# Six key-value iterations instead of seven, and the padding groups of edges at the end of a graph-transformer layer

## The chip, the cores and the metric

One core of a Trainium2 chip runs the whole layer as one program. Five engines work side by side: TensorE (PE, matmuls), VectorE (DVE), ScalarE (ACT), GpSimd (POOL, which here issues the gathers and scatters) and SyncE (SP, which issues plain transfers). The metric is the device time of one execution in microseconds, as the median of several runs.

## The reference

```
xn  = layernorm(x)                                   # 6250 nodes x 256
gnn = relu((relu(mean(xn[src] by dst) @ Wl.T + bl + xn @ Wr.T) @ Wln.T) + xn)   # 200000 edges
q, k, v = heads(xn @ w_qkv + b); k, v = layernorm(k), layernorm(v)     # 8 heads of 32
mix = gelu(((q @ (k.T @ v / 6250)) + xn) @ w1 + b1) @ w2 + b2 + xn
x   = x + gnn + mix
x   = x + shared_ffn(xn2) + top2_of_8_experts(xn2),  xn2 = layernorm(x)
```

The edges come sorted by destination, and low node numbers have more of them: in the inputs that `setup_inputs` draws, 40,621 of the 200,000 edges end in nodes 0 to 255, and 28,674 in nodes 0 to 127.

## The kernel before

**Tiles and groups.** The nodes are 49 tiles of 128 rows. The edges are cut into groups of 768 (6 columns of 128 edges); four groups, one for each buffer of `ring`, make an iteration, and 66 iterations cover 264 groups. The last edges, which belong to the highest nodes, are processed first. 261 groups hold real edges; three (`PADG`) hold only padding and are processed first, in iteration 0, from buffers set to zero.

**What a group costs.** POOL issues six indirect DMAs that gather 128 rows each of the normalised nodes `xn_d` into a ring buffer (`gather_edges`, L709). PE sums the rows by destination inside a window of 32 nodes (`window_sums`, L1734), DVE copies the sums (`keep_part`, L1223), PE places them in their tile (`place`, L1771), DVE adds them to the tile's sum (`finish`, L1158). When DVE has copied a group's sums it also copies the row numbers for a later gather (`next_rows`, L1231). A gather waits for that and, by the same register `group`, for `pass_`: the gather of group g may start when the sums of group g-3 are made.

**Stages.** First the node rows are normalised and stored to `xn_d`. In the *key-value stage* (`kv_iteration`, unrolled, iterations 0 to 6) each iteration handles four groups and seven node tiles, two tiles beside each of the first three groups and one beside the fourth (`SLOT`). A tile goes round ACT and DVE: ACT squares the projections (L843), DVE sums the squares (L1277), ACT takes the root, DVE the reciprocal and the product (L1283, L1286), ACT adds one (L831), PE multiplies keys by values (L1798). After tile 48 a short serial part makes the attention matrix (to L1433), and then the *node stage* starts, loops over iterations 7 to 65 on every engine.

**Node steps.** One iteration of the node stage does four groups and at most one *step* of the node work, which is a pipeline of steps 0 to 59: steps 0 to 51 finish one node tile after the other (SAGE, mixing, shared expert, from step 10 also pairs of row blocks of the routed experts), 52 is left out, step 53 opens the tables of the rest, and steps 54 to 59 do four single units of the routed experts each. A step may run only when no edge from this iteration on touches its tile: DVE makes a word for each iteration with the number of steps that are free, and `plan.look` sets `now` to the next step if its number is below that, and otherwise to `BLANK` (L93 to L96), which does nothing. With tile t the highest still touched, 48-t steps are free, three more when t is 1 or 0 and nine more when t is 0 (L1092 to L1095). After step 59 PE handles the last tile and its nine experts by itself.

**POOL's order.** In the node stage POOL's `step` issues, for each of the four buffers, the six gathers, and between them the step's two scatters of routed rows (L728) and two adds of expert results to the output (L737); for the single units one add for each buffer (L746). It is one queue in program order.

Of the kernel before, what the change touches and what calls it, by code (L numbers as in the profile page):

```python
# [8 lines left out]
ALU = mybir.AluOpType  # L9
# [4 lines left out]
ds = bass.ds  # L14

P = 128
NODES, D = 6250, 256
# [4 lines left out]
U = 6  # L22
RING = 4
KT = 7
KI = -(-NT // KT)
NKV = NT
SLOT = ((0, 1), (2, 3), (4, 5), (6,))
assert KI * KT == NT
NI = -(-EDGES // (P * U * RING))
# [3 lines left out]
SHELF = 8  # L33
# [168 lines left out]
def gps_layer(nc, x, idx, dst, wl, bl, wr, wln, wkv, bkv, wq, bq, kvg, kvb, w1, b1, w2, b2, wrt,  # L202
# [3 lines left out]
    with ctx:  # L206
# [216 lines left out]
        def rounds(it, b):  # L423

            return it if b < PADG else it + 1

# [30 lines left out]
        def _(sp):  # L457
# [8 lines left out]
            def first_lists():  # L466

                for b in range(RING):
                    sp.dma_start(idx_s[:, b, :], idx[RING * NI - 1 - b:RING * NI - b, :, :].squeeze(0)
                                 ).then_inc(S["idxin"], 16)  # L470

# [209 lines left out]
        def _(pool):  # L681
            nc.gpsimd.memset(ones_s[:, :], 1.0).then_inc(S["const"], 1)
            nc.gpsimd.memset(eps_s[:, :], EPS)
            nc.gpsimd.memset(zero_s[:, :], 0.0).then_inc(S["const"], 1)
            for b in range(PADG):
                nc.gpsimd.memset(ring[b][:, :, 0:D], 0.0)
            for b in range(RING):
# [11 lines left out]
            group = pool.alloc_register("group")  # L699
            pool.reg_mov(group, 2 + PADG)  # L700
            pool.sem_inc(S["idx"], RING + 1)
            pool.wait_ge(S["idxin"], 16 * RING)

            def gather_edges(b):
                pool.wait_ge(S["const"], 3)
                pool.wait_ge(S["idx"], group)
                pool.wait_ge(S["pass_"], group)
                for u in range(U):
                    pool.indirect_dma_start(  # L709
                        out=ring[b][:, u, 0:D], out_offset=None, in_=xn_d,  # L710
                        in_offset=IND(ap=idx_s[:, b, u:u + 1], axis=0)).then_inc(s_row[b], 16)
                pool.reg_add(group, group, 1)

            for b in range(PADG, RING):
                gather_edges(b)
            with pool.Fori(1, KI) as it:
# [32 lines left out]

            def step(gather):  # L750
                for b in range(RING):
                    if gather:
                        gather_edges(b)
                    if b == 1:
# [12 lines left out]
                with pool.If_lt(plan.single, plan.now):  # L767
                    pool.reg_add(units, units, 1)
# [11 lines left out]
            plan = Plan(pool, first=FIRSTS, second=SECONDS, add=ADDING, spread=SPREADING)  # L780
            with pool.Fori(KI, NI) as it:
                plan.look(word.now() >> RING)
                word.look_up(it + 1)
                step(True)
                plan.after()
            with plan.rest():
                with plan.left():
                    step(False)
                    plan.advance()
# [222 lines left out]
        def _(dve):  # L1012
# [27 lines left out]
            def extents():  # L1040

                dve.wait_ge(S["dstin"], 16)
                def pads_first(to):
                    V.tensor_copy(to[:, 0:2 * U], dst32_s[:, NG * U:])
                    return V.tensor_copy(to[:, 2 * U:], dst32_s[:, 0:NG * U])
# [21 lines left out]
            own.step(V.tensor_reduce(wide_s, span4_s, AX, ALU.max))  # L1067
            V.tensor_scalar(span_s[0:1, :], tile_i[0:1, :], 7, None, ALU.arith_shift_right).then_inc(S["span"], 1)
            dve.sem_inc(S["added"], 1)
# [29 lines left out]
            def pack(row, total, spare, terms):  # L1099
# [3 lines left out]
                for i, (part, factor) in enumerate(terms):  # L1103
# [104 lines left out]
            def enter_edges(edges):  # L1208

                finish(edges, -1)  # L1210
                state(edges, 1)
                narrow(edges, 1)
                with dve.If_eq(wide0, 1):
                    extra(at_group(edges[0], 0), edges[4][0])
                keep_part(edges, 0)
                dve.wait_ge(S["lists"], edges[0] * 16 + 16 * (len(SPANS) + 2 - SHELF))
                next_rows(edges[0] + 1, 0)
# [7 lines left out]
            def next_rows(it, b):  # L1225

                if isinstance(it, int):
                    at = shelf_of(it) * RING
                else:
                    at = dve.snap(shelf_of(it) * RING).with_bounds(min_val=0, max_val=(SHELF - 1) * RING)  # L1230
                V.tensor_copy(idx_s[:, b, :], lists_s[:, ds(at + (RING - 1 - b), 1), :].squeeze(1)).then_inc(S["idx"], 1)  # L1231

# [65 lines left out]
            def kv_iteration(it):  # L1298
                edges = begin(it)
                state(edges, 1)  # L1300
                for b in range(RING):
                    keep_part(edges, b)
                    next_rows(it + 1, b)
                    for j in SLOT[b]:
                        m = KT * it + j
                        if m:
                            scale(m - 1)
                        squares(m)
                        if j == SLOT[b][0] and (it, b) != (KI - 1, RING - 1):
                            finish(edges, b)  # L1310
# [404 lines left out]
        def _(pe):  # L1715
# [92 lines left out]
            def kv_iteration(it):  # L1808
                edges = begin(it)
                for b in range(RING):  # L1810
                    aggregate(edges, b)
                    for j in SLOT[b]:
                        m = KT * it + j
                        if m + 1 < NT:
# [4 lines left out]
                        if m >= 2:  # L1819
                            k_v(m - 2)  # L1820
                        if j == SLOT[b][0] and (it, b) != (KI - 1, RING - 1):
                            place(edges, b)
# [411 lines left out]
```

## Time and profile before

| | |
|---|---|
| median of 3 runs | 2538.97 us (2537.24 to 2541.27) |
| the profiled execution | 2541.11 us, of which 2539.1 us are its span |
| busy in the span | PE 2140.6 us (84%), POOL 1774.2 us (70%), DVE 1105.4 us (44%), ACT 769.8 us (30%) |
| gathers (L709) | 1566 DMAs, mean 956 ns |
| pieces of the gathers in the chain that ended last | POOL's issue 10%, the DMA itself 6% |

Busy time leaves out what an engine's sequencer does between instructions. A POOL that shows 70% can therefore still have a queue that never empties; the rows below show the idle time in front of each instruction, and what ended it.

### The profile page before, as it was taken

The numbers are of one execution on the slowest core, as the hardware profiler recorded it, in microseconds if no ns is written. First come the engines' busy times: TensorE is split into PE (matmuls) and PEld (weight loads), VectorE is DVE, ScalarE is ACT, GpSimd is POOL, SyncE is SP. The second block draws the span as 40 slices with busy tenths as digits, with TensorE's granted clock in tenths as the row PEclk, the third lists the DMA queues.
The fourth block names the chain that finished last, engine by engine and source line by source line (L and its number), as shares of the span: only waits on it lengthen the run. The fifth ranks groups of instructions, "written<-read, shape, count | busy, mean of one in ns | idle before, by whom it ended". The sixth has DMA issues, their size and how long they took to land.

```text
span 2539.1 us, 61133 instructions
## 1 busy us (share of the span) xinstructions
PE 2140.6 (84%) x13164; PEld 1655.5 (65%) x13165; DVE 1105.4 (44%) x4278; ACT 769.8 (30%) x1954; POOL 1774.2 (70%) x1786
## 2 busy tenths in 40 slices
PE   0888666777999999999999999999999866488979
PEld 0444445555777777777777777787777643377768
DVE  8555434444454445444444444444444322222321
ACT  4344222222233323323332333233333201022323
POOL 1477577777777777777777777777777777757720
PEclk9899778888999999999999999999999976599989
DMA  8333344445656665666566566656665654878834
GB/s 266 96 105 106 101 116 118 118 118 151 189 166 174 185 183 162 181 183 184 153 189 183 165 176 182 188 158 182 185 185 152 180 145 107 263 239 263 262 104 135
DMA packets 273733, 424.97 MB, mean 167 GB/s; under 512 B 76425, under 2 KB 202185, under 8 KB 272938
## 3 DMA queue, kind: packets, MB, share of 16 engines
q0 software_dynamic: 94880, 231.75, 33.6%
q1 hardware_dynamic: 172058, 183.19, 22.2%
q10 hardware_dynamic: 6384, 6.42, 0.7%
q14 instruction: 382, 3.13, 0.4%
q8 instruction: 29, 0.48, 0.1%
HBM read 380.74 MB, written 40.48 MB: 166 GB/s over the span
## 4 chain that ended last, share of the span: by engine, by line
PE 45%; issue 18%; POOL 13%; DVE 8%; DMA 7%; DVEq 4%; ACT 2%; SPq 1%; POOLq 1%; ACTq 0%
POOL region L709 10%; PE p_agg L1734 7%; PE p_y L1971 6%; DMA region<-xn_d,idx_s 6%; PE p_h L1960 4%; PE p_h L1927 4%; PE p_y L1933 4%; PE p_agg L1771 3%; PE p_h L2058 3%; PE p_a L2089 2%; PE p_t L1774 2%; PE p_a L1917 2%; POOL out_rows L737 2%; PE p_h L2123 1%; DVEq L171 1%
## 5 line engine op out<-in xcount | busy, mean ns | idle before, releaser
L709 POOL DMA_INDIRECT region<-xn_d,idx_s x1566 | 1497.3, 956 | 582.0 <-issue 447.6
L1734 PE MATMUL p_agg<-region,winhot 128*32 128x258 f32 x3168 | 318.0, 424 | 113.1 <-DMA region<-xn_d,idx_s 86.0
L1158 DVE TENSOR_TENSOR late<-late,p_agg 128x258 f32 x218 | 92.1, 423 | 514.9 <-issue 299.0
L1971 PE MATMUL p_y<-region 128*128 128x256 f32 x1280 | 293.5, 382 | 0.0
L1734 PEld LDWEIGHTS p_agg<-region,winhot 128*32 128x32 f32 x3168 | 120.3, 116 | 264.2 <-issue 197.9
L1771 PE MATMUL p_agg<-part_s,placehot 96*128 96x258 f32 x528 | 183.5, 431 | 119.7 <-DVE part_s L1223 95.7
L1971 PEld LDWEIGHTS p_y<-region 128*128 128x128 f32 x1280 | 240.1, 190 | 47.4 <-issue 16.6
L888 ACT ACTIVATE work<-p_h,b1s_s 128x128 f32<-128x128 f32 x384 | 109.7, 368 | 494.8 <-PE p_h L1927 494.8
L1960 PE MATMUL p_h<-wkv_s,region 128*128 128x256 f32 x960 | 229.2, 389 | 2.3 <-issue 2.2
L1960 PEld LDWEIGHTS p_h<-wkv_s,region 128*128 128x128 f32 x960 | 177.5, 191 | 40.8 <-issue 19.7
L1933 PE MATMUL p_y<-w2s_s,work 128*128 128x256 f32 x768 | 203.9, 390 | 0.0
L1927 PEld LDWEIGHTS p_h<-xft_s,w1s_s 128*128 128x128 f32 x1536 | 191.3, 200 | 11.0 <-issue 9.0
L1927 PE MATMUL p_h<-xft_s,w1s_s 128*128 128x128 f32 x1536 | 197.8, 284 | 0.0
L1771 PEld LDWEIGHTS p_agg<-part_s,placehot 96*128 96x128 f32 x528 | 91.1, 202 | 152.6 <-DVE part_s L1223 117.1
L1151 DVE TENSOR_TENSOR winhot<-row_s,iota_s 128x192 f32<-128x192 f32 (+1 forms) x265 | 95.1, 359 | 139.5 <-issue 131.6
L1933 PEld LDWEIGHTS p_y<-w2s_s,work 128*128 128x128 f32 x768 | 143.4, 197 | 18.3 <-issue 1.4
L737 POOL DMA_INDIRECT out_rows<-wkv_s,stok_s x80 | 130.0, 1625 | 24.4 <-issue 21.6
L870 ACT ACTIVATE region<-p_h,b_h 128x256 f32<-128x256 f32 x240 | 99.7, 471 | 151.0 <-PE p_h L1960 144.1
L1223 DVE COPY part_s<-p_agg 96x258 f32<-96x258 f32 x264 | 111.4, 422 | 62.2 <-PE p_agg L1734 47.8
L876 ACT ACTIVATE wkv_s<-p_t 128x512 f32<-128x512 f32 x40 | 23.9, 597 | 315.3 <-PE p_t L1774 315.3
L728 POOL DMA_INDIRECT slot_d<-xfp_s,posi_s x96 | 96.2, 1002 | 29.3 <-issue 27.7
L970 ACT ACTIVATE work<-p_h,b_h 128x128 f32<-128x128 f32 x192 | 55.0, 371 | 118.6 <-PE p_h L2058 81.7
(302 smaller groups left out, 3202.8 us busy)
## 6 DMA issues: line engine op xcount, KB each, us to landing
region<-in_w1p SPq DMA_DIRECT2D x60, 1024.0 KB, 7.3
region<-in_w2p SPq DMA_DIRECT2D x60, 1024.0 KB, 7.0
region<-xn_d,idx_s POOLq DMA_INDIRECT x1566
rows_s<-slot_d SPq DMA_DIRECT2D x40, 258.0 KB
region<-in_x SPq DMA_DIRECT2D x7, 896.0 KB, 12.7
xn_d<-region ACTq DMA_DIRECT2D x7, 896.0 KB, 4.1
rows<-in_x SPq DMA_DIRECT2D x49, 128.0 KB
xnr_s<-xn_d SPq DMA_DIRECT2D x49, 128.0 KB
```

What stands on the lines that cost most here:

```text
L709: pool.indirect_dma_start(out=ring[b][:, u, 0:D], out_offset=None, in_=xn_d, in_offset=IND(ap=idx_s[:, b, u:u + 1], axis=0)).then_inc(s_ro ...
L728: pool.indirect_dma_start(out=slot_d, out_offset=IND(ap=posi_s[:, k:k + 1], axis=0), in_=xfp_s[:, k, :], in_offset=None).then_inc(S["sc"], 16)
L737: pool.indirect_dma_start(out=out, out_offset=IND(ap=stok2_s[:, h:h + 1], axis=0), in_=yg2_s[:, h, :], in_offset=None, compute_op=ALU.add) ...
L870: nc.scalar.activation(hid2_s[:, j, :], h_wide[j], ACT.Gelu, bias=b1_h[0][:, j:j + 1]).then_inc(S["dgl"], 1)
L888: nc.scalar.activation(hid_s[:, j, :], h_one[j], ACT.Gelu, bias=b1s_s[:, j:j + 1]).then_inc(S["gl"], 1)
L1223: V.tensor_copy(part_s[0:QW, :], p_win).then_inc(S["part"], 1)
L1734: m = mm(p_win[j * WIN:(j + 1) * WIN, :], winhot[:, b % 2, PARTS[j][r], :], ring[b][:, PARTS[j][r], :], start=r == 0, stop=r == len(PARTS[ ...
L1771: mm(p_place, placehot[0:QW, b % 2, :], part_s[0:QW, :], start=True, stop=True).then_inc(S["placed"], 1)
L1927: m = mm(h_one[j], w1s_s[:, k, j * P:(j + 1) * P], xft_s[:, k, :], start=k == 0, stop=k == KD - 1)
L1933: m = mm(p_y[:, 0, :], hid_s[:, j, :], w2s_s[:, j, :], start=j == 0, stop=j == KF - 1)
L1960: m = mm(h_wide[j], w1p_s[0][:, c, j * P:(j + 1) * P], xgt_s[:, c, :], start=c == 0, stop=c == KD - 1)
L1971: m = mm(p_y[:, h, :], hid2_s[:, j, h * P:(h + 1) * P], w2p_s[0][:, j, :], start=j == 0 and h == 0, stop=j == KF - 1, skip_group_check=True)
```

## The change

`KI` goes from 7 to 6. The 49 tiles are spread over 24 slots: two tiles beside each group, three beside the last. The groups are turned by three places, so that the padding comes last: iteration 0 starts with real groups, and iteration 65 holds one real group and three of padding. The padding groups get the extent "tile 0" and window rows that match nothing, and their buffers are filled by one plain DMA each (`fill_padding`). The first four groups are gathered without a wait for `pass_`. POOL's loop ends at iteration 64; the last iteration is written out behind it. The row lists are read one iteration further ahead for three of the four buffers. The node stage starts with iteration 6; its steps and their conditions are as before.

```diff
-KT = 7
-KI = -(-NT // KT)
+KI = 6
-SLOT = ((0, 1), (2, 3), (4, 5), (6,))
+        def kv_tiles(it, b):
+            slot = RING * it + b
+            return range(slot * NT // (KI * RING), (slot + 1) * NT // (KI * RING))
...
-            for b in range(PADG):
-                nc.gpsimd.memset(ring[b][:, :, 0:D], 0.0)
...
-            pool.reg_mov(group, 2 + PADG)
+            pool.reg_mov(group, 2)
...
+            def fill_padding(b):
+                pool.wait_ge(S["const"], 3)
+                pool.wait_ge(S["idx"], group)
+                pool.wait_ge(S["pass_"], group)
+                pool.dma_start(ring[b][:, 0, 0:D], xn_d[0:P, :]).then_inc(s_row[b], 16 * U)
+                pool.reg_add(group, group, 1)
-            for b in range(PADG, RING):
-                gather_edges(b)
+            for b in range(RING):
+                gather_edges(b, free=True)
...
-            with pool.Fori(KI, NI) as it:
+            with pool.Fori(KI, NI - 1) as it:
                 plan.look(word.now() >> RING)
                 word.look_up(it + 1)
-                step(True)
+                step(RING)
                 plan.after()
+            plan.look(word.now() >> RING)
+            step(RING - PADG)
+            plan.after()
...
-            V.tensor_scalar(span_s[0:1, :], tile_i[0:1, :], 7, None, ALU.arith_shift_right).then_inc(S["span"], 1)
+            own.step(V.tensor_scalar(span_s[0:1, :], tile_i[0:1, :], 7, None, ALU.arith_shift_right))
+            for i in range(2):
+                last = V.memset(span_s[0:1, i * NS:i * NS + 2 + PADG], 0)
+            last.then_inc(S["span"], 1)
...
+            own.step(V.memset(rel_s[:, 0:(2 + PADG) * U], 255.0))
...
-                    for j in SLOT[b]:
-                        m = KT * it + j
+                    for m in kv_tiles(it, b):
```

On POOL, where the gathers start (after the reduction over partitions, `w2s_s`): before, six DMAs for the one real group of iteration 0, and then the loop of the key-value stage.

```order
L697 ISA w2s_s<-w1s_s 128x1596
L709 DMA region<-xn_d,idx_s 128x256 x6
L712 REGISTER_ALU
L716 UNCONDITIONAL_BRANCH
L709 DMA region<-xn_d,idx_s 128x256 x6
L712 REGISTER_ALU
```

The same place now:

```order
L697 ISA w2s_s<-w1s_s 128x1596
L710 DMA region<-xn_d,idx_s 128x256 x24
L713 REGISTER_ALU
L725 UNCONDITIONAL_BRANCH
L710 DMA region<-xn_d,idx_s 128x256 x6
L713 REGISTER_ALU
```

All four groups stand ahead of the loop, 24 DMAs without a wait between them.

On PE, the fourth group of iteration 0 (window sums `winhot`) up to the look at the next iteration's word: before, one tile (turn, project, keys by values) and the group's placing.

```order
L1734 MATMUL p_agg<-region,winhot 32x258 x6
L1774 MATMUL p_t<-id_s,region 128x128 x2
L1790 MATMUL p_h<-wkv_s,xt_s 128x512 x2
L1798 MATMUL p_y<-work 128x128 x2
L1771 MATMUL p_agg<-part_s,placehot 128x258
L1748 REGISTER_ALU
```

The same place now:

```order
L1754 MATMUL p_agg<-region,winhot 32x258 x6
L1794 MATMUL p_t<-id_s,region 128x128 x2
L1810 MATMUL p_h<-wkv_s,xt_s 128x512 x2
L1818 MATMUL p_y<-work 128x128 x2
L1791 MATMUL p_agg<-part_s,placehot 128x258
L1794 MATMUL p_t<-id_s,region 128x128 x2
L1810 MATMUL p_h<-wkv_s,xt_s 128x512 x2
L1818 MATMUL p_y<-work 128x128 x2
L1768 REGISTER_ALU
```

A second tile stands behind the placing; with it each iteration has eight tiles, the last of them nine.

On POOL, the written-out last iteration (new, behind the loop), from the gathers of its first buffer to the filling of the second and its neighbours:

```order
L710 DMA region<-xn_d,idx_s 128x256 x6
L713 REGISTER_ALU
L776 COMPARE_AND_BRANCH
L755 DMA out_rows<-late,stok_s 6400x256
L757 REGISTER_ALU
L776 UNCONDITIONAL_BRANCH
L720 DMA region<-xn_d 128x256
L721 REGISTER_ALU
```

Where the loop before has six gathers for each buffer, three buffers of this iteration have one plain DMA.

## Rows read from the trace of the kernel before

**Rows 1.** Page, part 1: busy us (share of the span) xinstructions.
```profile
PE 2140.6 (84%) x13164; PEld 1655.5 (65%) x13165; DVE 1105.4 (44%) x4278; ACT 769.8 (30%) x1954; POOL 1774.2 (70%) x1786
```

**Rows 2.** Waits of POOL's gathers: waited for, us in total, times, longest.
```profile
POOL region L709 <- issue: 447.6, 1468, 0.6
POOL region L709 <- PE p_agg L1734: 99.4, 63, 56.3
POOL region L709 <- DVE idx_s L1231: 30.2, 19, 16.6
```

**Rows 3.** Stretches: length, then each engine's busy us (xinstructions), PEclk, DMA share, GB/s.
```profile
95.80:299.90 204.10, 173.35 (x848) 94.22 (x847) 119.00 (x316) 93.60 (x189) 154.76 (x162) 0.92 0.39 111
316.30:617.70 301.40, 210.60 (x1373) 152.95 (x1373) 127.29 (x497) 75.31 (x196) 228.85 (x239) 0.80 0.41 116
617.70:1936.30 1318.60, 1243.71 (x7846) 1008.97 (x7846) 612.46 (x2574) 436.53 (x1115) 1012.08 (x1006) 0.98 0.61 177
1936.30:2207.60 271.30, 192.87 (x1066) 135.09 (x1065) 91.61 (x357) 45.53 (x121) 207.31 (x210) 0.78 0.59 175
2207.60:2413.00 205.40, 176.12 (x1210) 146.17 (x1213) 55.31 (x204) 50.08 (x171) 138.38 (x133) 0.94 0.80 246
```

**Rows 4.** POOL by line: busy us, mean ns, idle before and its releasers.
```profile
L737 POOL DMA_INDIRECT out_rows<-wkv_s,stok_s x80 | 130.0, 1625 | 24.4 <-issue 21.6 <-DVE xfp_s L1475 2.4 <-DMA out_rows<-rows 0.3
L728 POOL DMA_INDIRECT slot_d<-xfp_s,posi_s x96 | 96.2, 1002 | 29.3 <-issue 27.7 <-PE p_agg L1734 1.2 <-DVE idx_s L1231 0.3
L693 POOL DMA_DIRECT2D out_rows<-zero_s x2 | 1.3, 633 | 0.3 <-POOL region L688 0.3
```

**Rows 5.** SP's timeline: first issue behind its wait for the stored node rows.
```profile
52.06 0.36 SPq L503 DMA_DIRECT2D triu_s<-in_triu  x1
```

**Rows 6.** POOL's timeline, first gathers: start, us, ..., idle before and releaser.
```profile
82.17 1.07 POOL L709 DMA_INDIRECT region<-xn_d,idx_s  x1 [56.32 <-PE p_agg L1734]
...
89.02 0.95 POOL L709 DMA_INDIRECT region<-xn_d,idx_s  x1 [0.30 <-issue]
95.83 0.96 POOL L709 DMA_INDIRECT region<-xn_d,idx_s  x1 [5.86 <-PE p_agg L1734]
```

**Rows 7.** POOL's timeline between the key-value stage and the node stage.
```profile
298.70 0.95 POOL L709 DMA_INDIRECT region<-xn_d,idx_s  x1 [0.30 <-issue]
316.28 0.95 POOL L709 DMA_INDIRECT region<-xn_d,idx_s  x1 [16.63 <-DVE idx_s L1231]
```

**Rows 8.** DVE's timeline, sums of squares of four of the 49 tiles.
```profile
94.86 0.69 DVE L1277 TENSOR_REDUCE ve_s<-work 128x16 f32<-128x512 f32 x1 [1.36 <-ACT work L843]
...
98.27 0.69 DVE L1277 TENSOR_REDUCE ve_s<-work 128x16 f32<-128x512 f32 x1 [1.36 <-ACT work L843]
...
102.04 0.69 DVE L1277 TENSOR_REDUCE ve_s<-work 128x16 f32<-128x512 f32 x1 [1.36 <-ACT work L843]
...
287.07 0.69 DVE L1277 TENSOR_REDUCE ve_s<-work 128x16 f32<-128x512 f32 x1 [1.36 <-ACT work L843]
```

**Rows 9.** Line L1277: count, ns min/median/max, first and last start.
```profile
L1277 DVE TENSOR_REDUCE ve_s<-work x49: 685/685/687, 91.1 to 287.1; 128x16 f32<-128x512 f32 x49
```

**Rows 10.** PE's timeline, window sums of groups 23, 24, 26 and 28.
```profile
249.02 1.07 PE L1734 MATMUL p_agg<-region,winhot 128*32 128x258 f32 x12 [0.70 <-DMA region<-xn_d,idx_s]
...
256.40 1.85 PE L1734 MATMUL p_agg<-region,winhot 128*32 128x258 f32 x12 [0.76 <-DMA region<-xn_d,idx_s]
...
272.83 1.24 PE L1734 MATMUL p_agg<-region,winhot 128*32 128x258 f32 x12 [2.02 <-DMA region<-xn_d,idx_s]
...
313.51 1.94 PE L1734 MATMUL p_agg<-region,winhot 128*32 128x258 f32 x12
```

**Rows 11.** DVE's adds for groups that span two tiles.
```profile
L1251 DVE SCALAR_TENSOR_TENSOR late<-p_agg,upper_s,late 128x258 f32 x47 | 22.8, 484 | 101.5 <-issue 64.4 <-PE p_agg L1771 37.1
```

**Rows 12.** Line L709: count, ns min/median/max, first and last start.
```profile
L709 POOL DMA_INDIRECT region<-xn_d,idx_s x1566: 942/947/1200, 82.2 to 2420.9; - x196
```

**Rows 13.** PE's timeline, window sums of the last group, 263.
```profile
2439.76 1.07 PE L1734 MATMUL p_agg<-region,winhot 128*32 128x258 f32 x12
```

More of the change, by code:

```diff
@@ L23 @@
 RING = 4
-KT = 7
-KI = -(-NT // KT)
+KI = 6
 NKV = NT
-SLOT = ((0, 1), (2, 3), (4, 5), (6,))
-assert KI * KT == NT
 NI = -(-EDGES // (P * U * RING))
@@ L423, in rounds @@
         def rounds(it, b):
-            return it if b < PADG else it + 1
+            return it + 1
+        def kv_tiles(it, b):
+            slot = RING * it + b
+            return range(slot * NT // (KI * RING), (slot + 1) * NT // (KI * RING))
         def shelf_of(it):
@@ L468, in first_lists @@
                 for b in range(RING):
-                    sp.dma_start(idx_s[:, b, :], idx[RING * NI - 1 - b:RING * NI - b, :, :].squeeze(0)
-                                 ).then_inc(S["idxin"], 16)
+                    row = RING * NI - 1 - PADG - b
+                    sp.dma_start(idx_s[:, b, :], idx[row:row + 1, :, :].squeeze(0)).then_inc(S["idxin"], 16)
             def shelf_lists():
@@ L699, in _, with gather_edges @@
             group = pool.alloc_register("group")
-            pool.reg_mov(group, 2 + PADG)
+            pool.reg_mov(group, 2)
             pool.sem_inc(S["idx"], RING + 1)
             pool.wait_ge(S["idxin"], 16 * RING)
[L704 to L707, printed above, removed]
+            def gather_edges(b, free=False):
+                if not free:
+                    pool.wait_ge(S["const"], 3)
+                    pool.wait_ge(S["idx"], group)
+                    pool.wait_ge(S["pass_"], group)
                 for u in range(U):
@@ L712, in gather_edges @@
                 pool.reg_add(group, group, 1)
-            for b in range(PADG, RING):
-                gather_edges(b)
+            def fill_padding(b):
+                pool.wait_ge(S["const"], 3)
+                pool.wait_ge(S["idx"], group)
+                pool.wait_ge(S["pass_"], group)
+                pool.dma_start(ring[b][:, 0, 0:D], xn_d[0:P, :]).then_inc(s_row[b], 16 * U)
+                pool.reg_add(group, group, 1)
+            for b in range(RING):
+                gather_edges(b, free=True)
             with pool.Fori(1, KI) as it:
@@ L748, in add_single, with step @@
                 pool.reg_add(added, added, 16)
-            def step(gather):
+            def step(groups):
                 for b in range(RING):
-                    if gather:
+                    if b < groups:
                         gather_edges(b)
+                    elif groups:
+                        fill_padding(b)
                     if b == 1:
@@ L780, in _ @@
             plan = Plan(pool, first=FIRSTS, second=SECONDS, add=ADDING, spread=SPREADING)
-            with pool.Fori(KI, NI) as it:
+            with pool.Fori(KI, NI - 1) as it:
                 plan.look(word.now() >> RING)
                 word.look_up(it + 1)
-                step(True)
+                step(RING)
                 plan.after()
+            plan.look(word.now() >> RING)
+            step(RING - PADG)
+            plan.after()
             with plan.rest():
                 with plan.left():
-                    step(False)
+                    step(0)
                     plan.advance()
@@ L1043, in pads_first @@
                 def pads_first(to):
-                    V.tensor_copy(to[:, 0:2 * U], dst32_s[:, NG * U:])
-                    return V.tensor_copy(to[:, 2 * U:], dst32_s[:, 0:NG * U])
+                    V.tensor_copy(to[:, 0:(2 + PADG) * U], dst32_s[:, (NG - PADG) * U:])
+                    return V.tensor_copy(to[:, (2 + PADG) * U:], dst32_s[:, 0:(NG - PADG) * U])
                 own.step(pads_first(dst_s))
@@ L1215, in enter_edges @@
                 keep_part(edges, 0)
-                dve.wait_ge(S["lists"], edges[0] * 16 + 16 * (len(SPANS) + 2 - SHELF))
+                dve.wait_ge(S["lists"], edges[0] * 16 + 16 * (len(SPANS) + 3 - SHELF))
                 next_rows(edges[0] + 1, 0)
@@ L1225, in next_rows @@
             def next_rows(it, b):
+                ahead, b_list = divmod(b + PADG, RING)
                 if isinstance(it, int):
-                    at = shelf_of(it) * RING
+                    at = shelf_of(it + ahead) * RING
                 else:
-                    at = dve.snap(shelf_of(it) * RING).with_bounds(min_val=0, max_val=(SHELF - 1) * RING)
-                V.tensor_copy(idx_s[:, b, :], lists_s[:, ds(at + (RING - 1 - b), 1), :].squeeze(1)).then_inc(S["idx"], 1)
+                    at = dve.snap(shelf_of(it + ahead) * RING).with_bounds(min_val=0, max_val=(SHELF - 1) * RING)
+                V.tensor_copy(idx_s[:, b, :], lists_s[:, ds(at + (RING - 1 - b_list), 1), :].squeeze(1)).then_inc(S["idx"], 1)
             def finish(edges, b):
@@ L1299, in kv_iteration @@
                 edges = begin(it)
+                if it + 2 >= SHELF:
+                    dve.wait_ge(S["lists"], 16 * (len(SPANS) + it + 3 - SHELF))
                 state(edges, 1)
@@ L1308, in kv_iteration @@
                         squares(m)
-                        if j == SLOT[b][0] and (it, b) != (KI - 1, RING - 1):
+                        if m == kv_tiles(it, b)[0] and (it, b) != (KI - 1, RING - 1):
                             finish(edges, b)
@@ L1811, in kv_iteration @@
                     aggregate(edges, b)
-                    for j in SLOT[b]:
-                        m = KT * it + j
+                    for m in kv_tiles(it, b):
                         if m + 1 < NT:
@@ L1820, in kv_iteration @@
                             k_v(m - 2)
-                        if j == SLOT[b][0] and (it, b) != (KI - 1, RING - 1):
+                        if m == kv_tiles(it, b)[0] and (it, b) != (KI - 1, RING - 1):
                             place(edges, b)
```

## The prediction

> **What bounds the kernel now.** I read the page's busy line first: PE 84%, POOL 70% [rows 1]. That looks like a kernel bound by PE. The waits of POOL's gathers say otherwise: of 1566 gathers 1468 had in front of them only "issue", 447.6 us in all, 0.30 us each, and the longest was 0.6 us [rows 2]. So a gather takes 0.956 us and 0.30 us to issue, 1.257 us, and a group of six 7.54 us. Then the stretches [rows 3]: from 95.8 to 299.9 us POOL issues 162 gathers in 204.1 us, which is 1.260 us each; from 617.7 to 1936.3 us its 1006 instructions are busy 1012.1 us, and with 0.30 us in front of each that is 1313.9 of 1318.6 us. From 316.3 to 617.7 us the same sum gives 300.6 of 301.4 us, from 1936.3 to 2207.6 us 270.3 of 271.3 us. POOL is full in all four. Between them it has one real gap, 16.63 us before the gather at 316.28 us [rows 7]. So the clock of this kernel from 95.8 to 2207.6 us is POOL's queue, and time is lost or won there only when POOL stands idle or has more or less to issue. PE is busy 94% of 617.7 to 1936.3 us, close behind, but it is POOL that never waits.
>
> From 2207.6 us on that ends: 138.4 us busy and 133 times 0.30 us make 178.3 of 205.4 us. There the single units and their weights set the pace, and POOL runs ahead: the last gather is issued at 2420.9 us [rows 12], PE takes up the last group at 2439.8 us [rows 13].
>
> **The gap at 316 us.** The ring lets POOL run until group g waits for the sums of group g-3. When PE, ACT and DVE finish the key-value stage and then run the serial part, no sums are made; PE's first window sums of the node stage, of group 28, are at 313.51 us [rows 10], and POOL goes on with group 31 at 316.28 us.
>
> **What sets the end of the key-value stage.** The 49 sums of squares on DVE run from 91.1 to 287.1 us [rows 9]. Where nothing of a group comes between, one follows the other after 3.41 us (94.86 to 98.27), each time with 1.36 us of waiting for ACT's square; with a group's add and one-hots between, after 3.77 us (98.27 to 102.04) [rows 8]. That loop between ACT and DVE, not PE, is the floor: 48 intervals of 3.41 us are 163.7 of the 196.0 us. The other 32.3 us belong to the 27 groups that are finished beside them, with 3.5 us of waiting for gathers at groups 23, 24 and 26 (0.70, 0.76 and 2.02) [rows 10].
>
> **The change, part by part.**
>
> *Key-value stage.* The tiles stay 49, so 163.7 us stay. The groups finished beside them fall from 27 to 23. By the plain mean (32.3/27 = 1.20 us) that saves 4.8 us. If the 3.5 us of waiting for gathers, which the shorter row of groups should not have, are taken off first, a group costs 1.07 us, 23 cost 24.5 us, and the stage ends 7.8 us sooner. I take 6.5 us, near the middle; it has to cover as well the one step and three small memsets that DVE gets ahead of the stage, which no row shows and which I bound by 0 and 1 us. The first window sums of the node stage are then at 307.0 instead of 313.5 us, and POOL's release at 309.8 instead of 316.3 us. The serial part between, 26.4 us from 287.07 to 313.51 us [rows 8, 10], is the same.
>
> *What POOL has done by then.* Here the change loses. Before, POOL was at group 31 when it was released; now the first node iteration begins with group 24, so the release is for group 27. It was ready for it long before: from 95.83 us 23 groups of 7.54 us end at 269.3 us. Its idle time grows from 16.6 to 40.5 us. The four groups 27 to 30 that it had done before now follow the release, 4 x 7.54 = 30.2 us (step 0 has no scatter and no add), and group 31 comes at 340.0 us. The sum: 30.2 - 6.5 = **23.7 us later**.
>
> *Gathers at the start.* The stored rows are there at 52.06 us [rows 5], while the first gather before waited for PE until 82.17 us [rows 6]. The four free groups take 24 x 1.257 = 30.2 us and are done at 82.3 us, beside DVE's tables. They bring three real groups forward, but not the queue: group 4 still waits for the sums of group 1, whose end released it at 95.83 us after 5.86 us of idling, and these hang on DVE's and PE's first work. So 22.6 us of gathers are hidden here, and I cost this part at nothing; without that cover it would be up to 22.6 us.
>
> A rule of the skill speaks against that cover. The Trainium skill, page "SBUF — State Buffer", section "SBUF: two separate sides", says that GpSimd cannot write descriptors while DVE runs a copy in its two-port mode, and gives 3.1 us instead of 0.62 us for such a DMA. By that figure the 24 gathers would end at about 126 us, an estimate from that page. The trace has 1566 gathers beside all kinds of DVE work and none above 1.200 us [rows 12], against a median of 0.947; at that maximum the 24 end at 88 us, still under the cover.
>
> *The blocked iteration.* Steps now start at iteration 6, so step 46 would be due in iteration 52. Real groups run from the last to the first, and iteration 52 begins with edges 39,936 to 40,703. Only 40,621 edges end below node 256, so tile 2 is still touched, 46 steps are free, and step 46 is not below 46: iteration 52 does nothing but its groups. (The inputs drawn so have 47 groups that span two tiles, as many as DVE's rows [rows 11].) Steps 46 to 59 therefore run in the same iterations as before, 53 to 65. What iteration 52 spares POOL, two scatters of 1.00 and two adds of 1.63 us with 0.30 us each [rows 4], 6.5 us, it has issued an iteration sooner: up to iteration 53 POOL has the same scatters and adds, those of steps 0 to 45, and from group 4 on the same number of gathers. So the 23.7 us are neither grown nor shrunk at iteration 53, and pass through iterations 53 to 59, where POOL is full too [rows 3], to the opening of the tables, which waits for those groups.
>
> *The last iteration.* 18 gathers go (22.6 us of POOL), three plain DMAs come (0.63 us and 0.30 us each [rows 4], 2.8 us). But there POOL is 19 us ahead of PE, which does four units by then. I cost it at nothing; if PE did wait for POOL there, it would be 19.8 us won. Not taking it on the path is the nearer end, since PE's last window sums show no wait [rows 13].
>
> **The sum.** 2541.1 us of the profiled execution + 23.7 = 2564.8 us. The median of the runs is 2.1 us below that execution; I forecast **2562.5 us**, 0.9% slower. With 4.8 to 7.8 us for the key-value stage and 3 us to either side for the intervals of a fourth group with two tiles, which no row shows, its own range is 2556 to 2569 us. A measurement of this kernel tells 0.2%, 5.1 us, from no change.
>
> **Rivals.**
>
> *The gathers, not ACT and DVE, set the key-value stage.* Then the 49 tiles fit beside 24 groups at POOL's pace: group 23 at 249.0 us, as before, and its three tiles end 14.2 us later (272.83 to 287.07), at 263.3 us, 23.8 us sooner. The loss is 30.2 - 23.8 = 6.4 us: 2545.4 us. For it: at groups 23, 24 and 26 PE did wait for gathers [rows 10]. Against: with eight tiles an iteration needs 8 x 3.41 = 27.3 us and some 4.3 us for four groups, 31.6 us, more than POOL's 30.2.
>
> *PE, not POOL, bounds the node stage.* Then POOL's extra idling costs nothing, the node stage starts 6.5 us sooner, and the four groups that left the key-value stage fall into iteration 52, where PE has room: 2532.5 us, faster. For it: PE's 94%. It decides once an iteration needs 6% more of PE than now. Against: the 99.6% that POOL's instructions and issue times explain [rows 3].
>
> *The end pays.* If the last iteration was held by gathers, 19.8 us come back: 23.7 - 19.8 = 3.9 us, 2542.9 us. Against: 19 us of lead.
>
> *The steps aren't blocked.* If step 46 ran in iteration 52, the tables would open after 24 gathers less, 30.2 us, and a last iteration of four bare groups, about 10 us (an estimate: 1.94 us of sums for each [rows 10], and a little more than that for the copy, the placing and the hand-overs), would hang behind: 23.7 - 30.2 + 10 = 3.5 us, 2542.5 us. Against: the edge count, though by 83 edges only.
>
> *DVE holds up the early gathers.* A release of group 4 at 126 instead of 95.8 us costs between nothing and 30 us, as much as the sums of the next groups wait for it; with half of it the time is 2580 us. Against: the maximum of 1.200 us.
>
> **Chances.** The forecast 0.74, gathers in the key-value stage 0.08, PE as the bound 0.07, the end 0.05, unblocked steps 0.04, held-up gathers 0.02. The first, the second and the last are slower by over 0.2% (above 2544.1 us), 0.84, of which I move 0.01 to "within" because the second lies so near that bound; within 0.2% is then 0.10, faster 0.07. The range, 2544 to 2571 us, holds the first two and leaves out the rest.
>
> **What would show it.** Right: POOL's gathers from about 52 us, 24 in a row, then idle until about 96 us; in the key-value stage short waits of POOL for PE; one gap of about 30 to 40 us before the gather of the first node iteration at about 310 us; DVE's last sum of squares at about 280 us; iteration 52 with gathers but no scatter and no add on POOL; no more POOL gaps until the tables open, some 24 us later than before; and a last iteration with three plain DMAs, its units on PE as far apart as before. Wrong: a last sum of squares near 264 us (the gathers' pace), gaps on POOL in the node stage (PE's pace), scatters in iteration 52, or single units that come closer together at the end.

## The result: 0.9% slower

| | before | after |
|---|---|---|
| median (range), us | 2540.12 (2537.24 to 2545.53, 4 runs) | 2565.35 (2560.16 to 2566.97, 4 runs) |
| profiled execution, its span, us | 2541.11, 2539.1 | 2566.97, 2564.9 |

The ratio is 1.0093, 95% interval 1.0071 to 1.0116. The forecast was 2562.5 us, its own range 2556 to 2569 us. In the kernel after, line numbers are 1 to 20 higher: gathers L710 (L709 before), window sums L1754 (L1734), sums of squares L1296 (L1277), the add L1176, the part copy L1241.

The page's busy line of the kernel after, against [rows 1]:
```profile
PE 2142.2 (84%) x13164; PEld 1651.7 (64%) x13165; DVE 1108.4 (43%) x4281; ACT 766.5 (30%) x1954; POOL 1774.9 (69%) x1786
```
No engine has more to do. Nothing in this line shows 25 us. The waits of POOL's gathers, against [rows 2] (waited for, us in total, times, longest):
```profile
POOL region L710 <- issue: 460.0, 1505, 1.6
POOL region L710 <- PE p_agg L1754: 47.7, 39, 11.6
POOL region L710 <- DVE idx_s L1250: 43.7, 12, 35.4
```
The 56.3 us of waiting for PE before the first gather are gone (the gathers now begin at 53 us, behind 27.2 us of waiting for the stored rows), and a wait of 35.4 us stands where 16.6 us were. POOL's timeline shows both, against [rows 6, 7]:
```profile
53.18 1.06 POOL L710 DMA_INDIRECT region<-xn_d,idx_s  x1 [27.18 <-DMA xn_d<-region]
...
64.76 1.52 POOL L710 DMA_INDIRECT region<-xn_d,idx_s  x1 [0.30 <-issue]
66.58 2.03 POOL L710 DMA_INDIRECT region<-xn_d,idx_s  x1 [0.30 <-issue]
...
84.33 1.15 POOL L710 DMA_INDIRECT region<-xn_d,idx_s  x1 [0.31 <-issue]
96.88 0.95 POOL L710 DMA_INDIRECT region<-xn_d,idx_s  x1 [11.40 <-PE p_agg L1754]
...
275.14 0.95 POOL L710 DMA_INDIRECT region<-xn_d,idx_s  x1 [0.30 <-issue]
311.46 0.95 POOL L710 DMA_INDIRECT region<-xn_d,idx_s  x1 [35.38 <-DVE idx_s L1250]
...
341.69 0.95 POOL L710 DMA_INDIRECT region<-xn_d,idx_s  x1 [0.31 <-issue]
```
The 24 free gathers are done at 85.5 us and group 4 waits for PE until 96.9 us (95.8 before). Then POOL works up to 276.1 us, with three short waits for PE (1.2, 3.5 and 1.7 us), and stands until 311.5 us. That release is for group 27, as forecast; the one at 316.3 us before was for group 31.

The end of the key-value stage: line L1296 (count, ns min/median/max, first and last start), and PE's first window sums of the node stage, against [rows 9, 10]:
```profile
L1296 DVE TENSOR_REDUCE ve_s<-work x49: 685/686/689, 92.5 to 281.9; 128x16 f32<-128x512 f32 x49
```
```profile
308.70 1.94 PE L1754 MATMUL p_agg<-region,winhot 128*32 128x258 f32 x12
```
The 49 tiles take 189.4 us instead of 196.0, and the node stage's first sums come 4.8 us sooner, at 308.7 us. Group 31, the group that was released at 316.28 us before, is gathered from 341.7 us: 25.4 us later.

The stretches, against [rows 3] (length, then each engine's busy us (xinstructions), PEclk, DMA share, GB/s):
```profile
97.00:276.10 179.10, 156.32 (x765) 84.53 (x763) 103.47 (x263) 88.70 (x182) 131.79 (x138) 0.97 0.36 103
311.50:615.00 303.50, 210.59 (x1347) 151.74 (x1346) 126.94 (x489) 73.69 (x191) 230.66 (x240) 0.79 0.40 117
615.00:1963.00 1348.00, 1264.44 (x7981) 1018.87 (x7978) 625.25 (x2622) 442.09 (x1134) 1033.90 (x1030) 0.98 0.60 177
1963.00:2234.40 271.40, 183.16 (x1014) 126.80 (x1014) 85.63 (x334) 39.09 (x105) 207.42 (x210) 0.75 0.58 169
```
Add 0.30 us for each instruction of POOL, and behind the release it has 302.7 of 303.5, 1342.9 of 1348.0 and 270.4 of 271.4 us: full, as before. In the key-value stage it has 173.2 of 179.1 us, less full than before. Iteration 53's first gather comes at 1963.0 us instead of 1936.3, 26.7 us later. From group 31 to there both kernels take nearly the same time, 1621.3 us and 1620.0 before: the node iterations themselves have not become slower. PE's timeline, window sums of the last iteration's four groups, against [rows 13]:
```profile
2439.39 1.07 PE L1754 MATMUL p_agg<-region,winhot 128*32 128x258 f32 x12
2448.71 1.07 PE L1754 MATMUL p_agg<-region,winhot 128*32 128x258 f32 x12
2457.55 1.07 PE L1754 MATMUL p_agg<-region,winhot 128*32 128x258 f32 x12
2466.38 1.07 PE L1754 MATMUL p_agg<-region,winhot 128*32 128x258 f32 x12
```
The last are 26.6 us later than before, with no wait in front of any, and the span is 25.8 us longer. What is lost at 311 us is carried to the end.

POOL's timeline around iteration 52, from the last add before it to the first add of iteration 53:
```profile
1923.34 1.66 POOL L746 DMA_INDIRECT out_rows<-wkv_s,stok_s  x1 [0.30 <-issue]
1925.31 0.99 POOL L710 DMA_INDIRECT region<-xn_d,idx_s  x1 [0.31 <-issue]
...
1976.74 0.95 POOL L710 DMA_INDIRECT region<-xn_d,idx_s  x1 [0.30 <-issue]
1977.99 1.61 POOL L746 DMA_INDIRECT out_rows<-wkv_s,stok_s  x1 [0.30 <-issue]
```
There are 42 gathers between the two adds and neither a scatter nor an add among them. Iteration 52 itself runs from 1932.9 to 1963.0 us, 30.1 us, with nothing but gathers: the step is blocked.

### The profile page after: what moved, and what is told of

The parts are those of the page before. It is cut to its first block, busy times and chain, and to the rows that moved or that the text cites. A ratio compares the mean times of both kernels' runs of the same rounds, so it can differ in the third digit from the quotient of the medians.

```text
span 2564.9 us, 61319 instructions
## 1 busy us (share of the span) xinstructions
PE 2142.2 (84%) x13164; PEld 1651.7 (64%) x13165; DVE 1108.4 (43%) x4281; ACT 766.5 (30%) x1954; POOL 1774.9 (69%) x1786
## 4 chain that ended last, share of the span: by engine, by line
PE 40%; issue 23%; DVE 12%; POOL 9%; DVEq 7%; DMA 5%; ACT 2%; SPq 2%; POOLq 1%; ACTq 0%
POOL region L710 7%; PE p_y L1990 6%; PE p_agg L1754 5%; PE p_h L1946 5%; DMA region<-xn_d,idx_s 3%; PE p_agg L1791 3%; PE p_y L1952 3%; PE p_h L2077 3%; DVEq L168 2%; PE p_a L2108 2%; PE p_t L1794 1%; PE p_h L2142 1%; PE p_h L1979 1%; PE p_a L1919 1%; PE p_a L1921 1%
## 5 line engine op out<-in xcount | busy, mean ns | idle before, releaser
L710 POOL DMA_INDIRECT region<-xn_d,idx_s x1566 | 1500.4, 958 | 581.2 <-issue 460.0
L1754 PE MATMUL p_agg<-region,winhot 128*32 128x258 f32 x3168 | 315.5, 421 | 88.6 <-DMA region<-xn_d,idx_s 85.8
L1176 DVE TENSOR_TENSOR late<-late,p_agg 128x258 f32 x218 | 92.3, 423 | 540.6 <-issue 317.9
L1754 PEld LDWEIGHTS p_agg<-region,winhot 128*32 128x32 f32 x3168 | 118.7, 116 | 239.5 <-issue 194.9
L1791 PEld LDWEIGHTS p_agg<-part_s,placehot 96*128 96x128 f32 x528 | 91.1, 204 | 198.4 <-DVE part_s L1241 160.9
L746 POOL DMA_INDIRECT out_rows<-wkv_s,stok_s x80 | 130.0, 1625 | 24.4 <-issue 22.6
L1241 DVE COPY part_s<-p_agg 96x258 f32<-96x258 f32 x264 | 111.2, 421 | 52.5 <-PE p_agg L1754 35.8
```

Source lines behind the costliest of these rows:

```text
L710: pool.indirect_dma_start(out=ring[b][:, u, 0:D], out_offset=None, in_=xn_d, in_offset=IND(ap=idx_s[:, b, u:u + 1], axis=0)).then_inc(s_ro ...
L746: pool.indirect_dma_start(out=out, out_offset=IND(ap=stok2_s[:, h:h + 1], axis=0), in_=yg2_s[:, h, :], in_offset=None, compute_op=ALU.add) ...
L1241: V.tensor_copy(part_s[0:QW, :], p_win).then_inc(S["part"], 1)
L1754: m = mm(p_win[j * WIN:(j + 1) * WIN, :], winhot[:, b % 2, PARTS[j][r], :], ring[b][:, PARTS[j][r], :], start=r == 0, stop=r == len(PARTS[ ...
L1791: mm(p_place, placehot[0:QW, b % 2, :], part_s[0:QW, :], start=True, stop=True).then_inc(S["placed"], 1)
```

## The experiments

The theory was: POOL's queue is the clock of the node stage; six iterations instead of seven leave four more groups to gather behind the release; the order of the padding is worth nothing. Each ratio is to the kernel before, run on the same chip.

**One part alone, then the other.** e1 puts the padding last and keeps seven iterations:
```diff
-KI = 6
+KI = 7
```

> The changed kernel with KI = 7: padding last and early gathers stay, the key-value stage has seven iterations again. Theory 1 (POOL's queue is the clock; what costs is its idle time between the stages, which four groups fewer in the key-value stage made longer): idle back to 15 to 19 us, step 53 in iteration 59 as before, 18 gathers off the end without worth; 2538 to 2546 us, the same as before. Rival 'order' (turning the groups costs): about 2565 us. Rival 'end' (early gathers and a light last iteration are worth their 20 us): about 2520 us.

Measured: 2544.84 us, 1.0014 (1.0005 to 1.0024). The gap in POOL's timeline is before group 31 again (19.7 us, 15 to 19 expected):
```profile
317.07 0.95 POOL L710 DMA_INDIRECT region<-xn_d,idx_s  x1 [19.69 <-DVE idx_s L1250]
```
e2 is the kernel before, padding first, with six iterations and the tiles spread over them:
```diff
-KT = 7
-KI = -(-NT // KT)
+KI = 6
...
-                    for j in SLOT[b]:
-                        m = KT * it + j
+                    for m in kv_tiles(it, b):
...
```

> The kernel before with KI = 6 and the tiles spread over 24 slots, padding first as before. Theory 1: idle of 35 to 41 us between the stages; iteration 52 begins with edges up to 43,007, so it is blocked as well; 2560 to 2570 us, like the change. Rival 'order': 2541 us, since the padding isn't moved. Rival 'PE bounds the node stage': 2530 to 2541 us.

Measured: 2566.84 us, 1.0094 (1.0079 to 1.0109). POOL's long gap between the stages in its timeline is before group 27, as in the kernel after (33.3 us, a little under the 35 to 41 expected):
```profile
308.56 0.95 POOL L711 DMA_INDIRECT region<-xn_d,idx_s  x1 [33.25 <-DVE idx_s L1233]
```
The six iterations alone cost all of it; the rest of the change (the order of the padding, the early gathers) costs 0.1% without them.

**POOL's queue as the clock.** e7 adds to the kernel before one gather of 128 rows that nobody uses in each of 59 node iterations:
```diff
...
+                        if b == 3:
+                            pool.wait_ge(S["const"], 3)
+                            pool.wait_ge(S["spare"], spare)
+                            pool.indirect_dma_start(out=spare_p[:, :], out_offset=None, in_=xn_d,
+                                                    in_offset=IND(ap=spare_i[:, 0:1], axis=0)).then_inc(S["spare"], 16)
+                            pool.reg_add(spare, spare, 16)
```

> The kernel before with one more indirect gather on POOL in each of the 59 node iterations (128 rows into a buffer that nobody reads; the result doesn't change). Theory 1: 1.257 us for each of the 53 iterations 7 to 59, 67 us, and little in the last six: 2600 to 2615 us. Rival 'PE bounds the node stage': under 10 us more, 2540 to 2550 us.

Measured: 2605.61 us, 1.0247 (1.0231 to 1.0262), 65 us more. The added line (count, ns min/median/max, first and last start), then what POOL waited for in front of it:
```profile
L764 POOL DMA_INDIRECT spare_p<-xn_d,spare_i x59: 945/949/1059, 323.7 to 2490.0; - x59
```
```profile
POOL spare_p L764 <- issue: 17.4, 57, 0.3
```
59 times (0.949 + 0.30) us are 73.7 us; without the six behind the opening of the tables, where POOL has time to spare, 66.2, and 65 were measured. Had PE been the clock, it would have hidden them. That POOL's queue sets the node stage up to the opening of the tables is shown.

**One group further ahead.** e5 takes from the kernel before POOL's own wait for the sums of group g-3; the wait for the index list, which DVE copies behind the sums of group g-4, stays.
```diff
-                pool.wait_ge(S["pass_"], group)
```

> The kernel before, gathers wait for the list of row numbers alone (DVE writes it when it has copied the sums of group g-4) and no longer for the sums of group g-3: POOL may run one group further ahead. Theory 1: the release at 316 us is for group 32 instead of 31, POOL's idle time there falls from 16.6 to about 9 us, and all behind it is 7.5 us sooner: 2530 to 2535 us. Rival 'PE bounds the node stage': no change, 2540 us. Rival (the gathers' landing, not their issue, is late): no change either.

Measured: 2535.88 us, 0.9978 (0.9969 to 0.9987), the fastest kernel here, but 4.3 us under its before and not 7.5. POOL's gap in its timeline, and its wait in front of the first scatter behind it:
```profile
316.83 0.95 POOL L708 DMA_INDIRECT region<-xn_d,idx_s  x1 [15.25 <-DVE idx_s L1230]
...
374.87 1.01 POOL L727 DMA_INDIRECT slot_d<-xfp_s,posi_s  x1 [4.07 <-DVE xfp_s L1474]
```
The gap now stands before group 32, so one group more is done when POOL stops. It is 15.25 us long and not 9, since the queue had started sooner (group 4 at 87.6 us instead of 95.8). Group 32 is gathered 7.0 us sooner than in the kernel before (323.8 us), but group 40 only 2.2 us sooner (385.1 and 387.3): on the way POOL waits 4.1 us for DVE before its first scatter, where it did not wait before, and 1.6 us for a list. So a lead of the queue is kept only up to the next thing that POOL waits for. e8 does the same to e1; `fill_padding` keeps its wait.

> e1 (seven iterations, padding last) with the wait of e5 left out. Theory 1: as e5, 2530 to 2536 us, since the order of the padding has no price of its own. Rival 'order' or 'end': off from e5 by 20 us to one side or the other.

Measured: 2537.77 us, 0.9993 (0.9984 to 1.0002): no difference from before, and a little over the 2530 to 2536 us expected. It is 2.4 us under its before, e1 2.2 us over its own, so the wait is worth 4.6 us here. The gap stands before group 32, as in e5.

**The blocked iteration.** e4 moves the 448 padding edges of the partial group to the end as well, so that tile 2 is free in time, and resets one bound of the plan of steps, so that the singles follow the tables without a pause:
```diff
...
-    src[:EDGES] = v["src"]
+    src[LEAD:LEAD + EDGES] = v["src"]
...
-    dst[:EDGES] = v["dst"]
+    dst[:LEAD] = v["dst"][0]
+    dst[LEAD:LEAD + EDGES] = v["dst"]
```

> The changed kernel with the 448 padding edges of the partial group moved to the end too (all edges shift by 448 places), so iteration 52 starts with edges 39,488 to 40,255 and step 46 isn't blocked; steps 46 to 59 run in iterations 52 to 64, and iteration 65 has only groups. Theory 1: POOL idles as long as in the change (35 us), but the tables open 24 gathers, 30.2 us, sooner, and four bare groups of 10 to 15 us hang behind the last units: 2543 to 2552 us. Rival (the blocked iteration costs nothing, since some engine other than POOL has the same work in it): 2565 us, no change against the change.

Measured: 2560.44 us, 1.0065 (1.0053 to 1.0078), 8 us above the range expected. The step was unblocked and DVE starts on the tables 24.9 us sooner (at 2161.9 instead of 2186.8 us), but little of that is left at the end: e4 is 17.8 us over its before, the kernel after 25.2 us over its own, with intervals that overlap, and the spans of the profiled executions are 1.5 us apart (2563.4 and 2564.9). PE's timeline of e4 behind its last unit:
```profile
2448.55 1.89 PE L2114 MATMUL p_a<-region,work 128*128 128x256 f32 x8
...
2458.86 1.23 PE L1797 MATMUL p_agg<-part_s,placehot 96*128 96x258 f32 x2 [5.86 <-DVE part_s L1247]
...
2467.29 1.94 PE L1760 MATMUL p_agg<-region,winhot 128*32 128x258 f32 x12
2471.84 1.23 PE L1797 MATMUL p_agg<-part_s,placehot 96*128 96x258 f32 x2 [2.61 <-DVE part_s L1247]
2480.94 0.66 PE L1800 MATMUL p_t<-id_s,xnr_s 128*128 128x128 f32 x2 [7.87 <-DVE mean_s L1467]
```
The last unit ends at 2450.4 us (2474.9 in the kernel after, 24.4 us later), but the bare iteration that now hangs behind it lasts until the last placing at 2473.1 us: 22.6 us, with PE waiting for DVE's copies. In the kernel after PE has single units to run between these copies. So the 24.4 us are given back but for 1.8. In all these kernels seven of 66 iterations carry no step; before, all seven lie in the key-value stage. The change brings one of them out of it, and it is paid for in the middle or at the end. e6 is e4 without the wait that e5 removes.

> e4 (six iterations, all padding last, step 46 not blocked) with the wait of e5 left out. Theory 1: 7.5 us less than e4, so 2536 to 2545 us. Rivals as for e5: as e4.

Measured: 2558.74 us, 1.0062 (1.0049 to 1.0076), a miss: against its own before it is no better than e4 (1.0065), where 7.5 us were expected. POOL stops before group 28 instead of 27 and gathers group 32 at 343.6 us, 4.3 us sooner than in e4 (347.9), but it too waits for DVE before its first scatter (3.4 us), and at group 100 nothing is left (942.5 and 942.4 us).

**Five iterations, and a miss.** e3 is the kernel after with one number changed:
```diff
-KI = 6
+KI = 5
```

> The changed kernel with KI = 5 (20 groups beside the 49 tiles). Theory 1: the stage ends another 4 to 6 us sooner, the release is for group 23 instead of 27, so POOL idles 60 to 66 us there and everything behind is another 24 to 26 us later; steps wait in iterations 51 and 52; 2585 to 2595 us. Rival 'PE bounds the node stage': 4 to 6 us less than the change, 2560 us. Rival 'transition is a fixed cost of the change': 2565 us.

Measured: 2703.18 us, 1.0628 (1.0611 to 1.0645), over 100 us beyond the theory's time. The release is for group 23 and comes 5.9 us sooner than in the kernel after (305.6 us), both as expected, and group 31 comes 27.1 us later (368.8 us). POOL's idle time before the release is 34.5 us and not 60 to 66, since POOL already stands at eight of the groups 6 to 21, 2.9 to 5.6 us each. So the rest of the loss lies in the node stage. From 1000 to 1500 us, what PE waited for, first in the kernel after, then in e3:
```profile
PE p_agg L1791 <- DVE part_s L1241: 9.3, 9, 2.3
```
```profile
PE p_agg L1791 <- DVE part_s L1241: 39.7, 13, 3.8
```
and what POOL's gathers waited for PE there, after and e3:
```profile
POOL region L710 <- PE p_agg L1754: 2.4, 8, 0.3
```
```profile
POOL region L710 <- PE p_agg L1754: 17.5, 10, 3.4
```
In e3 PE waits 3 us in each iteration for DVE's part copy, once, at the top of the node loop. PE's timeline at one such place, after and e3:
```profile
1003.52 0.70 PE L1791 MATMUL p_agg<-part_s,placehot 96*128 96x258 f32 x2 [1.49 <-DVE part_s L1241]
```
```profile
1049.64 1.23 PE L1791 MATMUL p_agg<-part_s,placehot 96*128 96x258 f32 x2 [3.49 <-DVE part_s L1241]
```
Behind a pause of 3.5 us the placing takes 1.23 us, not 0.70; the mean granted clock of the stretch is 0.93 of 2.4 GHz in e3 and 0.99 in the kernel after. So POOL, which hardly waited for PE, waits for it. DVE's timeline there, after and e3:
```profile
996.36 0.14 DVE L1495 TENSOR_SCALAR xfp_s<-rv_s 128x1 f32<-128x1 f32 x1
1002.06 0.42 DVE L1176 TENSOR_TENSOR late<-late,p_agg 128x258 f32 x1 [5.56 <-issue]
...
1003.05 0.41 DVE L1241 COPY part_s<-p_agg 96x258 f32<-96x258 f32 x1
```
```profile
1040.55 0.14 DVE L1495 TENSOR_SCALAR xfp_s<-rv_s 128x1 f32<-128x1 f32 x1
1048.15 0.42 DVE L1176 TENSOR_TENSOR late<-late,p_agg 128x258 f32 x1 [7.46 <-issue]
...
1049.16 0.42 DVE L1241 COPY part_s<-p_agg 96x258 f32<-96x258 f32 x1
```
DVE itself waits for "issue": its sequencer has jumped back to the loop's first instruction. From 1000 to 1900 us, in the mean, it resumes 3.4 us behind the jump in the kernel after (24 iterations) and runs on; in e3 it resumes after 3.0 us, and six or eight instructions later stops again for 2.3 us (in all 23 iterations). The semaphore that the next instruction waits for was set 12.6 us earlier at the place shown. The trace has packets of an instruction queue, 8 KB each (82 packets, 0.67 MB in 500 us of the kernel after; it doesn't say for which engine).
```diff
+            for _ in range(n):
+                dve.sem_inc(S["spare"], 1)
```

> The five-iteration stage (e3_five) with 20 semaphore increments, which nobody waits for, at the start of VectorE's program: they move all of VectorE's later code by 20 instructions and change nothing else. In the trace of e3_five VectorE needs 5.7 to 6.7 us from the jump at the end of its node loop to the first add (in the changed kernel 4.0 to 4.7), with a second stop of 1.9 to 3.1 us some nine instructions behind the loop's start; TensorE waits 2.7 to 3.9 us for the part copy behind that add in each iteration (1.5 to 2.3 in the changed kernel), and node iterations take 39.2 us (36.7). Theory 1 (the code's place decides: the loop's first instructions lie across two blocks of fetched code): the second stop is gone, the first add comes under 5 us behind the jump, node iterations are POOL's again at 36.7 us, and the time is 2585 to 2610 us. Rival (five iterations themselves cost it, by the steps that start sooner or by the other engines' phases): the second stop or the wait of TensorE stays, and the time stays at 2695 to 2715 us.

> The changed kernel with 81 such increments at the start of VectorE's program, so that its node loop starts at the same place within 128 instructions as in e3_five. Theory 1: the second stop appears in VectorE's loop head, the first add comes 5.5 to 7 us behind the jump instead of 4.0 to 4.7, TensorE waits about 3 us and more for the part copy, node iterations become about 39.2 us instead of 36.7, and the time is 2640 to 2690 us. Rival (the place of the code is nothing to the node iterations): 2560 to 2570 us, as the changed kernel.

Measured: e9 2606.72 us, 1.026 (1.0234 to 1.0287); e10 2649.89 us, 1.0405 (1.0369 to 1.044). PE's wait for the part copy in the same stretch, e9 and e10, then POOL's for PE, e9 and e10:
```profile
PE p_agg L1793 <- DVE part_s L1243: 25.6, 14, 2.9
```
```profile
PE p_agg L1793 <- DVE part_s L1243: 32.6, 13, 3.2
```
```profile
POOL region L710 <- PE p_agg L1756: 4.0, 9, 1.6
```
```profile
POOL region L710 <- PE p_agg L1756: 23.9, 17, 3.1
```
The same instructions 20 places on are 96 us faster, 81 places on 85 us slower; of the 85 us 2.8 are there already at the release (314.2 us), as the increments also take time at the start. The mean time from DVE's last payload instruction to the part copy (620 to 1900 us, 32 to 35 iterations) is 6.9 us in the kernel after, 7.2 in e9, 7.8 in e10 and 8.3 in e3: the order of their times beyond what the iterations cost. In e10 one thing differs from what I expected: the add comes in time (3.8 us behind the jump in the mean), and the second stop (1.4 to 2.2 us, in 19 of 23 iterations) stands right behind it, still ahead of the part copy. The packets go with the stops here too: two in the one stop of all 25 jumps of e9, and in e10 one in the first stop and one in each second one.
With the code moved, five iterations cost 66 us over before and 41 us over six: nearer to the 2585 to 2595 us that the first theory gave for e3, and still 12 us and more above them. Up to group 40 e9 is 26.3 us behind the kernel after, as the theory has it; between groups 40 and 100 another 12.7 us are lost, where POOL waits for PE (8.5 us instead of 3.0) and for DVE before scatters, and behind that almost nothing. The remainder has a place but no tested cause.

## Why the prediction was right, by its own steps

- *POOL's queue is the clock:* right for the node stage, by e7 and by the three stretches behind the release. In the key-value stage it no longer is: there POOL now waits for PE at times, as the signs to look for had it.
- *Key-value stage 6.5 us shorter:* right in length, 6.6 us (196.0 to 189.4). The start slipped by 1.4 us (first sum of squares 92.5 instead of 91.1), more than the 0 to 1 us that I allowed for DVE's added work, and the forecast places are all some 2 us early: last sum 281.9 (280), first node sums 308.7 (307.0), release 311.5 (309.8). What made the start slip was not tested.
- *Release for group 27, 30.2 us behind:* right. The sum +23.7 us is +25.4 us measured at group 31 and +25.8 us in the span; of the 1.7 us more 1.4 are that slip, and the rest is the part from the last sum of squares to the release, 29.6 us instead of 29.2. POOL's idle time was put at 40.5 us and is 35.4: it was not done at 269.3 us but, with its waits for PE, at 276.1. That changes nothing in the time, because the loss hangs on when the release comes and on what is left behind it, not on how long POOL stood.
- *Gathers at the start cost nothing:* right, with less room. The bound of 1.200 us for one gather was wrong: two of the 24, beside DVE's wide table instructions (128x798 and 128x1596), took 1.52 and 2.03 us. The rule of the Trainium skill, page "SBUF — State Buffer", section "SBUF: two separate sides", which I had set against the cover, may show there, at less than its 3.1 us and for two gathers, not 24; no run tests the cause.
- *Iteration 52 blocked, nothing grown or shrunk there:* blocked, as forecast; 30.1 us of gathers. From group 31 to iteration 53 the delay grows by 1.3 us, more than nothing; it does not shrink by 30 us, as in the rival of unblocked steps.
- *The last iteration costs and gains nothing:* right. PE's window sums of its four groups lie 9.3, 8.8 and 8.8 us apart; before they lay 9.4, 8.8 and 8.8 us apart (2412.72 to 2439.76).
- *Rivals.* Gathers as the pace of the key-value stage would have ended it at 263 us, PE as the bound would have swallowed the gap; neither happened. The rival of unblocked steps was mis-sized: it put the bare iteration at the end at 10 us, and e4 shows 22.6, with PE waiting for DVE's copies and its clock at 0.68 of 2.4 GHz from 2440 to 2480 us. With 22.6 us, and with the 24.4 us by which the units really come sooner, its sum is 23.7 - 24.4 + 22.6 = 21.9 us: 2561, not 2542.5 us.

## What to carry to other kernels

Look for the queue that never waits for anybody, its issue time counted in; work moved to an earlier stage pays only if that queue gets further by it, and starting a later stage sooner loses when the queue has less behind it at the handover. Count the iterations that must run without the other work; moving one out of a stage where it was hidden only chooses where it is paid. Before a size change is judged, see whether it has moved a loop's code, by looking at how long the engine takes from the jump to the first instructions that others wait for.

## What was not expected of the hardware

The place of DVE's code alone is worth 85 to 96 us, 3 to 4%, in these kernels. The jump to the node loop's start costs DVE 2.8 to 3.8 us in the mean of every kernel looked at, and a second stop adds 1.4 to 3.1 us in most iterations of the two that start at place 115. DVE, busy 43% of the span, shows nothing of it in its share: it becomes a wait of 2.5 to 3 us for PE in each iteration, a lower granted clock behind it, and from iteration 25 to 50 one iteration takes 39.5 us in e3 and 38.5 in e10 instead of 36.8 in the kernel after.
